# Moving the exchange of the RNN's weight maxima, ScalarE's copy of the LSTM bias and one of VectorE's maxima by one tick, in an RNN followed by an LSTM

## The reference

```python
def _L0(x, h0, Wx, Wh, b):            # RNN
    xW = einsum('ntd,dh->nth', x, Wx) + b
    h = tanh(h_prev @ Wh + xW_t)      # h0 = cond_1024

def _L1(x, h0, Wx, Wh, b):            # LSTM, c0 = 0
    a = x_t @ Wx + b + h_prev @ Wh    # 512 -> 2048: i, f, o, g
    c = sigmoid(f) * c_prev + sigmoid(i) * tanh(g)
    h = sigmoid(o) * tanh(c)          # h0 = cond_1024

x = x + _L0(x, cond_1024, ...)
x = x + _L1(x, cond_1024, ...)
```

## Time and profile before

| | us |
|---|---|
| median of 3 runs | 835.91 (835.72 to 837.06) |
| the profiled execution | 834.66 |
| its span | 832.9 |

### The profile page before, as it was taken

The page is one execution under the profiler, slowest core; times in us unless marked ns, Lnnn a source line. Parts: engine busy times, 40 slices in busy tenths (PEclk is TensorE's granted clock), DMA queues, the critical chain, the costliest instruction groups (busy, mean ns, idle before and its releaser), DMA issues.

```text
span 832.9 us, 52087 instructions
## 1 busy us (share of the span) xinstructions
PE 821.0 (99%) x22614; PEld 612.0 (73%) x22614; DVE 651.6 (78%) x1800; ACT 607.5 (73%) x1632; POOL 335.2 (40%) x693
## 2 busy tenths in 40 slices
PE   8999999999999999999999999999999999999997
PEld 4556556677788877778777787777777778777796
DVE  4798788887988878878787887878878787767764
ACT  3985577776777777777877778787787878777752
POOL 1421466846544343343534434343343434333320
PEclk9999999999999999999999999999999999999999
DMA  8711100111011111111111111111111101010001
GB/s 309 269 37 28 30 16 28 29 29 26 12 26 29 29 40 29 33 41 36 50 29 37 24 41 41 35 47 33 29 30 43 42 21 37 18 32 21 13 14 28
DMA packets 54580, 36.21 MB, mean 43 GB/s; under 512 B 9788, under 2 KB 52944, under 8 KB 53072
## 3 DMA queue, kind: packets, MB, share of 16 engines
q1 hardware_dynamic: 54096, 32.78, 14.2%
q10 hardware_dynamic: 256, 0.11, 0.0%
HBM read 19.21 MB, written 8.39 MB: 33 GB/s over the span
## 4 chain that ended last, share of the span: by engine, by line
PE 90%; DVE 4%; DMA 2%; ACT 2%; issue 1%; SPq 0%; POOL 0%; ACTq 0%; DVEq 0%; POOLq 0%
PE ps_l L1639 36%; PE ps_l L1734 29%; PE ps_r L1862 9%; PE ps_l L1681 4%; PE ps_pk L1845 3%; PE ps_r L1882 2%; PE ps_end L1845 2%; PE ps_l L1653 2%; DMA whl_raw<-in_L_cond_Wh 2%; PE ps_l L1673 1%; DVE whl_lo L1385 1%; DMA wxr_raw<-in_L_cond_Wx 1%; PE ps_l L1626 0%; PE ps_r L1793 0%; PE ps_r L1804 0%
## 5 line engine op out<-in xcount | busy, mean ns | idle before, releaser
L601 POOL TENSOR_TENSOR xb<-xb,h_l 128x128 f32<-128x128 f32 x127 | 58.0, 457 | 370.8 <-DVE h_lo L1445 368.5
L1734 PE MATMUL ps_l<-whl_raw,wxl_raw 128*32 128x256 f16 x3816 | 131.6, 273 | 0.0
L1639 PE MATMUL ps_l<-whl_hi,hT_hi 128*32 128x512 f16 x1888 | 122.5, 379 | 0.4 <-DVE hT_hi L1429 0.4
L1639 PE MATMUL ps_l<-whl_hi,hT_lo 128*32 128x512 f16 x1888 | 122.6, 379 | 0.0
L1639 PE MATMUL ps_l<-whl_lo,hT_hi 128*32 128x512 f16 x1888 | 122.5, 379 | 0.0
L1734 PE MATMUL ps_l<-wxl_hi,wxl_raw 128*32 128x256 f16 x2544 | 115.7, 273 | 0.0
L1734 PEld LDWEIGHTS ps_l<-whl_raw,wxl_raw 128*32 128x32 f16 x3816 | 102.1, 97 | 2.2 <-issue 0.2
L1639 PEld LDWEIGHTS ps_l<-whl_hi,hT_lo 128*32 128x32 f16 x1888 | 51.1, 97 | 50.7
L1639 PEld LDWEIGHTS ps_l<-whl_lo,hT_hi 128*32 128x32 f16 x1888 | 50.9, 97 | 51.0
L1013 ACT ACTIVATE gates<-ps_l,g_products 128x256 f32<-128x256 f32 x115 | 53.8, 468 | 42.4 <-PE ps_l L1639 42.2
L1734 PEld LDWEIGHTS ps_l<-wxl_hi,wxl_raw 128*32 128x32 f16 x2544 | 68.4, 97 | 17.4 <-issue 0.2
(11 more groups left out here) (270 smaller groups left out, 1917.0 us busy)
## 6 DMA issues: line engine op xcount, KB each, us to landing
xb<-in_x SPq DMA_DIRECT2D x128, 64.0 KB, 2.1
out<-xb SPq DMA_DIRECT2D x124, 64.0 KB, 1.9
whl_raw<-wxl_lo SPq DMA_DIRECT2D x160, 32.0 KB, 2.1
whl_raw<-in_L_cond_Wh SPq DMA_DIRECT2D x4, 1024.0 KB, 6.5
wxl_raw<-in_L_cond_Wx SPq DMA_DIRECT2D x4, 1024.0 KB, 5.8
wxr_raw<-in_L_cond_Wx SPq DMA_DIRECT2D x1, 1024.0 KB, 5.6
whr_raw<-in_L_cond_Wh SPq DMA_DIRECT2D x1, 1024.0 KB, 7.5
wxl_raw<-in_L_cond_b SPq DMA_DIRECT2D x1, 256.0 KB, 3.5
```

What stands on the lines that cost most here:

```text
L601: nc.gpsimd.tensor_tensor(xb[g % NX][:, t, :], xb[g % NX][:, t, :], h_l[s % 2][:, :], ALU.add).then_inc(out_done, 1)
L1639: last = nc.tensor.matmul(ps_l[s % 4][quarter(j), :], (hT_hi, hT_lo)[h_part][:, k, :], gate_slice(whl[w_part][k], j), start=False, stop=(h ...
L1734: last = nc.tensor.matmul(at[quarter(j), :], stationary, weights[:, j, :, :], start=False, stop=(y_part == 1 and k == 1), skip_group_check ...
```

## The change

The exchange of the RNN's maxima is moved one tick down on all engines (TensorE turns in tick 2 and spreads in tick 3; VectorE reduces in tick 2, takes the result and makes the scales in tick 3). ScalarE's bound of WhR stays in tick 0. ScalarE's copy of the LSTM bias goes from tick 0, where it stood ahead of this bound, to tick 1, right ahead of the seed that is made from it. VectorE's maximum of WhL's chunk 0 goes from behind the turn of tick 0 to behind the turn of tick 1.

```diff
-        R_SCALE_AT = 1
-        R_STEPS_AT = 2
+        R_SCALE_AT = 2
+        R_STEPS_AT = 3
@@ ScalarE, loop over ticks
-                if k == 0:
+                if k == 1:
                     bias_of_l()
-                if k == 1:
                     seed_step_0()
@@
-                if k == R_SCALE_AT - 1:
+                if k == 0:
                     rnn_weight_bound()
```

## The result

| | before | changed |
|---|---|---|
| median of 22 executions each | 836.86 | 837.18 |
| lowest to highest | 834.89 to 837.77 | 835.72 to 839.24 |
| the profiled execution, its span | 834.66, 832.9 | 838.17, 836.4 |

The ratio is 1.0015, 95% interval 1.0009 to 1.0021. The change makes the kernel slower, by 0.15% or 1.25 us: inside the range and inside the 0.2% that I called "same", but clear of noise in this measurement, where "all hidden, no difference" was the forecast. The rival with the falling clock happened. The size is less sure than the direction: the two medians differ by 0.32 us, the two means (837.44 and 836.54) by 0.90. That 837.18 lies so near the rival's 837.3 is luck, since the kernel before took 836.86 here and not the 835.91 that I had started from.

What follows compares the result with a forecast made beforehand. TensorE, busy 821.0 of 832.9 us, was taken as the bound, its steady part set by a chain that is DMA alone until 21.22 us. Terms 0 + 0 + 0 + 0 left the median at 835.9 us, range 835.0 to 837.4.

Steps and rivals of the forecast that it cites:

- same: Whole kernel: no difference beyond about 0.2%, 1.7 us, which a measurement can tell from no change; chance 0.90.
- all hidden, no difference: Whole kernel: every moved step costs and gains 0, median stays 835.9 us; chance 0.80.
- The rival with the falling clock: TensorE's clock falls in a lengthened hole before 20.41 us; +1.4, at most +2.2 us, 837.3 to 838.1; chance 0.08.
- Parts 1 to 3: Ticks 0 to 3: bias copy, WhL chunk 0 maximum and RNN maxima exchange moved later; each 0 on the chain.
- Part 4: TensorE in tick 3 loses 0.65 to 1.01 us to late x group and spreading matmuls; taken as 0, at worst +0.2.

Runs made afterwards that it cites:

- changed, filled: Changed kernel plus matmuls with unused results: 8 in tick 2, ratio 1.0003 to the kernel before; 8 in tick 2 and 2 in tick 1, 0.9994.
- its two parts alone: Kernel before with only the bias copy and maximum moved, ratio 1.0006; kernel before with only the exchange moved one tick down, ratio 1.0003.
- the kernel before with the piece in tick 3: Kernel before with the first piece of step 0's recurrent product moved from tick 2 to tick 3 on TensorE; ratio 1.0008.
- the one with the longest hole: Changed kernel with the first piece of step 0's recurrent product moved from tick 2 to tick 3; ratio 1.0025 to the kernel before.
- the first measurement: Changed kernel against the kernel before, 22 executions each, medians 837.18 and 836.86 us; ratio 1.0015; the kernel before's clocks not on record.
- the three groups: Follow-up kernels, each group with its own runs of the kernel before, which averaged 835.95, 835.97 and 835.92 us.
- the pair of 1.0025 and 0.9997: Changed kernel with step 0's first piece moved to tick 3, ratio 1.0025; the same with 12 unused-result matmuls in tick 2, 0.9997.
- the exchange alone: Kernel before with the exchange of the RNN's maxima moved one tick down, bias copy and maximum left in tick 0; ratio 1.0003.

## Why the prediction was wrong

**Parts 1 to 3, right, in the trace at full clock and in the fallen one.** The tanh of tick 1 came at 14.44 (14.38 forecast) and the turn at 14.73. The tanh of tick 2 stayed behind the bound that waited 2.01 us for the DMA. The exchange held the x group on VectorE. That all this is worth 0 on the chain is shown by yardsticks of 21.66 (before), 21.66 and 21.67 (changed, filled) and 21.68 and 21.67 (its two parts alone), all at full clock.

**Part 4, right at full clock.** The late x group made TensorE wait 0.25 to 0.53 us in tick 3, the spreading matmuls came on top, and the idle 0.46 us ahead of tick 4 took it up. The idle 0.34 ahead of the LSTM's product was not needed: it is 0.44 and 0.52 us in the filled traces.

**The rival, its chance: this is the step that failed.** I saw the hole, put it at 2.2 us (2.63 and 2.40 in the traces), set it between 1.30 us where nothing fell and 3.8 us where it fell, and then gave it 0.08 with no reason for so low a number. A point between two ends, one of which falls, asked for something near an even chance. Measured: 21 of 34 executions. I also took the trace of before as proof that its own hole was safe, though it was one execution; 13 of 103 fall. With such a chance the forecast of the mean would have been half the price, not 0.

**The rival, its price: mis-sized.** I took 4.4 us at half clock from the start of the kernel, and +1.4 us, at the most +2.2. The profiled fall ran at 0.50 through all of 22 to 28 us and cost 2.47 on the yardstick (2.54 in the other), because the idle 0.46 us of tick 3, which I had counted against the fall, had gone to the late x group and the spreading matmuls already, and the half clock lasted longer than I took. By the stretches, a fall lasted 6.8 us in three traces (both of the changed kernel, and the kernel before with the piece in tick 3) and 3.4 us in the one with the longest hole; none lasted 4.4. The shorter fall cost about 0.5; the one in the kernel before with the piece in tick 3 gave 45.05 - 22.05 = 23.00, 1.34 above, of which a part may be the piece's place. Averaged over executions a fallen one of the changed kernel is 1.1 to 1.6 us above a kept one (837.14 - 836.02, 837.88 - 836.26). In the first measurement the 9 executions with a mean clock of 0.995 or less took 838.4, the other 7 fallen ones 837.2, the kept ones 836.3: a long fall costs more there than a short one.

**The sum as it should have been.** Where both kernels ran beside each other with their clocks on record, the clock fell in 0.42 of the executions (5 of 12) instead of 0.06 (2 of 33). The difference of 0.36 times 1.1 us gives 0.4 us; the means differ by 0.52 (836.49 and 835.97), and the ratio of 1.0003 can't be told from 1. For the first measurement the sum can't be made, because the share of falls in the kernel before isn't known there. If it had been 0.13, as in the three groups, 0.73 - 0.13 = 0.60 times 1.6 us would give 1.0 us, beside the 0.90 by which the means differ and the 1.25 of the ratio; the slower kernel before speaks for a larger share and so for less. How much of the 1.25 us is the clock's stays open. I can't separate it from the scatter of the shares.

What the Trainium skill says of it ("TensorE: Matmul & The Clock Gate", Part 1: activity is what releases the throttle) was set down as a risk in the prediction; the pair of 1.0025 and 0.9997 agrees with it.

**Open.** Whether the hole ahead of tick 2 (1.21 us in its trace) or the one ahead of tick 3 (1.11) makes the clock fall in 5 of 11 with the exchange alone, and how long they were in the executions that fell: these were timed, not profiled. Nor is it shown which hole, tick 1's or tick 2's, the falls of the kernel before come from. A late chunk 0 lengthens tick 1's: to 1.58 us in one trace, which kept its clock, and to 2.11 in another, which lost it.

## What to carry to other kernels

While an engine waits for loads, moving its work earlier gains nothing and can open a hole where TensorE used to be busy; count TensorE's busy time in every stretch after such a move, not only the chain. A hole that is known to be safe in one trace is known for one execution; compare many executions by their mean clock, and both kernels in the same rounds. If such a hole can't be closed with real work, a few matmuls whose result is not used close it: with the longest hole they turned 1.0025 into 0.9997. In the kernel before, whose clock falls seldom, no gain from them was measured.

## What the runs showed of the hardware that I had not expected

The kernel whose trace has a stretch of 3.25 us without a matmul dropped TensorE to its lower level (1.2 of 2.4 GHz) in 11 executions of 11, the one whose traces have 2.40 and 2.63 us in 21 of 34; the shortest wait ahead of a fall in a trace is 2.11 us. The price depends on the execution as well: full clock was back by 24 us in one trace (3.4 us at 1.2 GHz) and only after 28 us in two others (6.8 us), about 0.5 and 2.5 us on the chain.
